# Splitting norm, statistics and last-square blocks of two attention layers into phases of a lane

## The chip, the cores and the metric

The program runs on one core of one Trainium2 chip. The core has five engines that work at the same time, each through an instruction queue of its own: TensorE (PE; matmuls and transposes into PSUM banks), VectorE (DVE), ScalarE (ACT; functions such as square root, Silu and exponential, and copies out of PSUM), GpSimd (POOL) and SyncE (SP; transfers). An instruction that needs another engine's result waits on a semaphore at the head of its own queue. The metric is the device time of one execution of the whole program in microseconds (us); lower is better.

## What is computed

The reference is four layers, each an attention and a feed-forward part, on 8 sequences of 512 rows of 128 columns. The change touches the first and the third attention. Both are gated "delta rules" over normed rows. Cut to what matters here:

```python
# first attention (4 heads of 32 columns; x is layer-normed)
q, k, v = silu(causal_conv(x @ Wq)), silu(causal_conv(x @ Wk)), silu(causal_conv(x @ Wv))
beta = sigmoid(x @ Wb)
q, k = l2norm(q), l2norm(k)                 # per row and head: x * rsqrt(sum(x * x))
kb, v = k * beta, v * beta
out = delta_rule_chunkwise(q, k, v, kb)     # triangular inverse per chunk, then a scan over chunks
short, long = fir(v_direct, 5 taps), fir(v_direct, 64 taps)
stats = [mean, var, abs_mean, l2] of each of (short, long, out, v_direct)   # per row and head
weights = softmax(gelu([x, stats] @ W1 + b1) @ W2 + b2)
x = x + rmsnorm(mix of the four branches by weights) @ Wo

# third attention (4 heads; q, k of 32 columns, v of 64)
q, k, v = silu(causal_conv(h @ Wq)), silu(causal_conv(h @ Wk)), silu(causal_conv(h @ Wv))
q, k = l2norm(q) * 32 ** -0.5, l2norm(k)
g, beta = -exp(A) * softplus(h @ Wa + dt), sigmoid(h @ Wb)
o = gated_delta_rule(q, k, v, g, beta)
x = x + (rmsnorm(o) * silu(h @ Wg)) @ Wo    # then a small feed-forward part
```

## The kernel before

The program is a row of stages, one for each attention or feed-forward part. All engines meet at the start of a stage. In an attention stage one unit of work is one sequence: 512 rows as four tiles of 128, on 128 partitions. Eight units go through **two lanes**: lane 0 takes units 0, 2, 4, 6 and lane 1 units 1, 3, 5, 7, so a stage consists of four pairs. Each lane has its own buffers and four PSUM banks (`b[0]` to `b[3]`).

What sets the order of the work is the function `weave`. Every engine has a generator for a unit (`pe`, `act`, `dve`, `pool` of a stage's class) that issues instructions and yields the name of a phase: what is issued before a `yield` belongs to the phase of that name. `weave` takes one phase of lane 0 and one phase of lane 1 in turn, with lane 0 one phase ahead (`lead=1`), the same on each engine. So between two phases of lane 0 an engine's queue holds exactly one phase of lane 1, which is the one before in the list. Each engine runs its queue in this order, and dependences between engines are waits for named steps (`wait_ge(*u.act.at("norms"))`).

In the first attention (`L0Attn`) the phases are stats, features, project, convolve, rows, keys, then for two pairs of chunks the delta rule (score, strict, left and right levels, turn, wt, u, out), then branches, squares, statistics, gate, hidden, logits, softmax, mix, out, end. The parts concerned are:

- **rows**. PE turns the three convolved tensors and the early v into rows (line 422, called from `pe`). ACT copies them (lines 1169 and 1171), squares keys and queries (1173, 1174), waits for DVE's sums and takes the root (1176). DVE waits for the key squares, reduces (1301), waits for the query squares, reduces (1303), multiplies v by beta (1306), waits for the root, and forms reciprocal (1308) and the products of keys and queries (1310, 1311, 1313; step `ready`). PE's transposes of the phase keys wait for `ready`; ACT copies those (1179, 1182) and moves the held product (1184), and then PE can form the scores (782) and, after the strict part, the levels (801, 809). In the phase convolve, DVE's four multiply-adds per tensor stand at lines 1294 and 1297, and ACT applies Silu (1165).
- **branches and squares**. In the phase branches ACT copies the short filter's rows (1203). In the phase squares it squares the four branches (1208), waits for all statistics, and takes the root of the lengths (1210). `statistics_dve` does four blocks of eight instructions (1385 to 1397), one block for each branch, all in the phase squares. PE turns the statistics, ACT copies them (1213), PE forms the gate's products (1128) and DVE adds (1346).

The third attention (`L2Attn`) has the same shape. Its rows phase has ACT's copies (2736, 2739), squares (2741, 2742) and root (2744), DVE's reductions (2846), v product (2852), reciprocal (2855) and products (2857 to 2860). Between convolve and rows lies a phase decays (ACT's exponential at 2732); keys has ACT's copies at 2747 and 2750 and DVE's weighing (2864, 2865), and the first phase of the delta rule starts with DVE's step masks (2869). At a unit's end, in the phase squares, ACT squares the output (2770) and takes the root (2772); DVE reduces (2904), applies the gates (2908), and scales (2910, 2912). Then PE turns the rows and projects (2685), and DVE adds (2917).

## Time and profile before

| what | value |
|---|---|
| median of 3 runs | 5995.02 us (5983.47 to 5996.26) |
| the profiled execution: its own time, and its span | 5991.27 us, 5989.9 us |
| PE busy | 4244.2 us, 71% of the span |
| DVE busy | 2997.1 us, 50% |
| ACT busy | 1940.4 us, 32% |
| POOL busy | 817.9 us, 14% |
| share of the chain that ended last | PE 50%, DVE 29%, ACT 12% |
| first attention, about 28 to 1060 us | PE 790.2, DVE 484.1, ACT 311.4 us busy of 1032; mean granted clock 0.55 |
| third attention, about 2880 to 3920 us | PE 709.2, DVE 552.4, ACT 326.5 us busy of 1040; mean granted clock 0.62 |

No engine is busy for the whole span, so the shares say little alone. The way to read this profile is by stage, and in a stage by place: a row of the timeline gives the start and the duration of a merged group of instructions, its engine, line and shapes, and in brackets how long the engine had been idle before it and what ended that. The granted clock is a share of 2.4 GHz: 0.5 is 1.2 GHz.

### The profile page before, as it was taken

The numbers are of one execution on the slowest core, as the hardware profiler recorded it, in microseconds if no ns is written. First come the engines' busy times: TensorE is split into PE (matmuls) and PEld (weight loads), VectorE is DVE, ScalarE is ACT, GpSimd is POOL, SyncE is SP. The second block draws the span as 40 slices with busy tenths as digits, with TensorE's granted clock in tenths as the row PEclk, the third lists the DMA queues.
The fourth block names the chain that finished last, engine by engine and source line by source line (L and its number), as shares of the span: only waits on it lengthen the run. The fifth ranks groups of instructions, "written<-read, shape, count | busy, mean of one in ns | idle before, by whom it ended". The sixth has DMA issues, their size and how long they took to land.

```text
span 5989.9 us, 94866 instructions
## 1 busy us (share of the span) xinstructions
PE 4244.2 (71%) x39740; PEld 3259.9 (54%) x39740; DVE 2997.1 (50%) x7965; ACT 1940.4 (32%) x4236; POOL 817.9 (14%) x600
## 2 busy tenths in 40 slices
PE   6786968467888888855485766857777677776288
PEld 5574947345655555544374655734444445445277
DVE  4445363335455555565446555465555555555333
ACT  2233132123333333311323233234444444442122
POOL 0000000221100111124200000011111111110443
PEclk6555555688789988866666666668887788778599
DMA  9100000230000000011200000000000000000265
GB/s 261 41 2 1 2 1 2 87 119 1 1 1 1 1 1 1 1 35 19 48 2 1 1 1 1 2 1 1 1 1 1 1 1 1 1 1 1 67 167 139
DMA packets 140861, 152.33 MB, mean 25 GB/s; under 512 B 7809, under 2 KB 128003, under 8 KB 139793
## 3 DMA queue, kind: packets, MB, share of 16 engines
q1 hardware_dynamic: 119024, 128.21, 7.4%
q0 software_dynamic: 21408, 18.05, 1.8%
q8 instruction: 313, 5.13, 0.4%
q14 instruction: 116, 0.94, 0.1%
HBM read 87.38 MB, written 59.76 MB: 25 GB/s over the span
## 4 chain that ended last, share of the span: by engine, by line
PE 50%; DVE 29%; ACT 12%; issue 3%; POOL 2%; DMA 2%; another core or an unknown queue 1%; SPq 0%; DVEq 0%; POOLq 0%; ACTq 0%
PE banks_lane L801 4%; ACT work L3231 4%; PE banks_lane L422 3%; PE banks_lane L3668 2%; PE banks_lane L1885 2%; PE banks_lane L3073 2%; PE banks_lane L1251 2%; PE banks_lane L809 2%; PE banks_lane L3117 2%; PE banks_lane L950 1%; DVE weights L3324 1%; ACT work L1979 1%; PE banks_lane L3152 1%; DVE work L2793 1%
## 5 line engine op out<-in xcount | busy, mean ns | idle before, releaser
L422 PE MATMUL banks_lane<-constants,work 128*128 128x128 f32 x968 | 203.9, 361 | 513.7 <-DVE work L408 231.5
L422 PEld LDWEIGHTS banks_lane<-constants,work 128*128 128x128 f32 x968 | 155.9, 187 | 587.2 <-DVE work L408 222.6
L402 POOL TENSOR_TENSOR weights<-weights,constants 128x4 f32<-128x4 f32 x76 | 78.5, 1033 | 2088.9 <-DVE weights L397 2088.9
L422 PE MATMUL banks_lane<-constants,weights 128*128 128x128 f32 x596 | 124.5, 347 | 336.3 <-DVE weights L408 98.0
L3231 ACT ACTIVATE work<-banks_lane,weights 128x192 f32<-128x192 f32 (+1 forms) x512 | 248.2, 499 | 245.9 <-DVE weights L3328 245.9
L422 PEld LDWEIGHTS banks_lane<-constants,weights 128*128 128x128 f32 x596 | 88.6, 178 | 369.6 <-issue 169.7
L3336 POOL TENSOR_TENSOR weights<-weights,constants 128x16 f32<-128x16 f32 x64 | 185.4, 2896 | 531.0 <-DVE weights L3244 531.0
L402 POOL TENSOR_TENSOR work<-work,constants 128x4 f32<-128x4 f32 x76 | 77.3, 1018 | 1192.3 <-DVE work L397 1192.3
L3152 PE MATMUL banks_lane<-constants,work 128*128 128x128 f32 x896 | 149.5, 316 | 120.5 <-DVE work L3316 70.7
L3152 PEld LDWEIGHTS banks_lane<-constants,work 128*128 128x128 f32 x896 | 113.1, 160 | 150.3 <-DVE work L3316 89.0
L2032 DVE TENSOR_REDUCE work<-banks_lane 128x2 f32<-128x512 f32 x256 | 158.8, 683 | 67.7 <-PE banks_lane L1899 67.3
L3324 DVE TENSOR_REDUCE weights<-banks_lane 128x2 f32<-128x384 f32 (+1 forms) x256 | 121.9, 518 | 114.6 <-PE banks_lane L3139 114.1
L1979 ACT ACTIVATE work<-banks_lane 128x384 f32<-128x384 f32 (+1 forms) x256 | 118.5, 550 | 174.9 <-PE banks_lane L1920 106.9
L3080 PE MATMUL banks_lane<-constants,weights 128*128 128x128 f32 x256 | 68.4, 419 | 139.1 <-DVE weights L3255 82.6
L3668 PE MATMUL banks_lane<-weights,work 128*128 128x256 f32 x624 | 143.1, 382 | 14.7 <-DVE weights L3710 14.7
L3167 PE MATMUL banks_lane<-work 128*64 128x128 f32 x1792 | 127.8, 284 | 34.0 <-ACT work L3193 34.0
L656 POOL DMA_INDIRECT out<-weights,chunk_places x78 | 121.5, 1557 | 194.4 <-DVE chunk_places L648 127.3
L569 POOL DMA_INDIRECT room_l_ffn<-weights,indices x96 | 92.6, 965 | 397.3 <-DVE weights L392 341.3
L3073 PE MATMUL banks_lane<-weights,work 128*128 128x512 f32 x192 | 145.0, 918 | 0.0
L801 PE MATMUL banks_lane<-work 64*64 64x32 f32 x2048 | 124.2, 293 | 23.4 <-DVE work L891 19.6
L1885 PE MATMUL banks_lane<-weights,work 128*128 128x128 f32 x1024 | 135.5, 297 | 5.9 <-ACT work L2001 5.9
L1885 PEld LDWEIGHTS banks_lane<-weights,work 128*128 128x128 f32 x1024 | 131.3, 211 | 10.3 <-ACT work L2001 10.3
(779 smaller groups left out, 11145.2 us busy)
## 6 DMA issues: line engine op xcount, KB each, us to landing
work<-experts_dram_l_ffn SPq DMA_DIRECT2D x39, 964.0 KB
room_l_ffn<-work SPq DMA_DIRECT2D x30, 1188.0 KB, 15.1
work<-experts_dram_l_ffn SPq DMA_DIRECT2D x23, 512.0 KB
weights<-weights_dram SPq DMA_DIRECT2D x1, 4833.5 KB, 14.3
work<-room_l_ffn SPq DMA_DIRECT2D x36, 132.0 KB, 3.2
weights<-weights_dram SPq DMA_DIRECT2D x1, 4112.0 KB, 12.7
weights<-bands_dram SPq DMA_DIRECT2D x1, 4096.0 KB, 13.1
weights<-room_l_ffn SPq DMA_DIRECT2D x26, 132.0 KB, 4.4
```

The source lines that it names most:

```text
L402: pool.tensor_tensor(n.rstd, n.rstd, c("neghalf", cols=(0, n.rstd.shape[1])), ALU.pow).then_inc(*u.pool.step(name))
L422: done = pe.transpose(bank[0:rows, t * P:(t + 1) * P], block, c("ident"))
L801: made = pe.matmul(b[2][g, m * SMALL:(m + 1) * SMALL], self.strict[g, m, :], self.x[g, m, :])
L1885: made = pe.matmul(b[1][:, cols_of(t)], m.ff[:, f, cols_of(t)], self.w(u, f"down{f}"), start=f == 0, stop=f == L1_ATTN_FF - 1)
L1979: act.activation(m.probs[:, hh, 0:blocks, :].rearrange("p b q -> p (b q)"), b[hh][:, 0:blocks * P], ACT.Exp, scale=L1_ATTN_SCALE).then_inc ...
L2032: dve.tensor_reduce(m.top[r][:, :, hh, L1_ATTN_HD], b[hh][:, :].rearrange("p (t c) -> p t c", t=2), AX, ALU.max, negate=True).then_inc(*u. ...
L3073: pe.matmul(b[n][:, :], m.xT[:, cols_of(t)], self.w(u, "qkv", cols=(n * L2_FFN_INNER, (n + 1) * L2_FFN_INNER))).then_inc(*u.pe.step(f"proj ...
L3152: made = pe.transpose(u.banks[2 + side][:, cols_of(hh)], m.probs[n % 2][:, hh, side * P:(side + 1) * P], self.c("ident"))
L3231: act.activation(m.probs[n % 2][:, hh, L2_FFN_BACK + lo:2 * P], u.banks[side][:, j * span:(j + 1) * span], ACT.Exp, scale=m.q_factor[:, t, ...
L3324: dve.tensor_reduce(m.top[:, t, 4 * group + side:4 * group + 4:2], u.banks[side][:, 0:2 * span].rearrange("p (j c) -> p j c", j=2), AX, AL ...
L3336: pool.tensor_tensor(m.rn[:, t, :, :], m.rn[:, t, :, :], c("neghalf", cols=(0, 2 * L2_FFN_HEADS)).rearrange("p (n h) -> p n h", n=2), ALU. ...
L3668: made = pe.matmul(bank[:, g * CHUNK:(g + 1) * CHUNK], self.w(u, f"{name}{f}", cols=(g * P, (g + 1) * P)), m.z[:, f, :], start=f == 0, sto ...
```

## The change

Only `yield` statements are added, at the same places of all four engines' generators. No instruction is added, removed or altered, except for table loads of ACT, which the build puts in where the function changes.

- In both attentions rows becomes three phases: **squared** (PE's transposes, ACT's copies and squares), **summed** (DVE's two reductions and the v product, ACT's root) and **rows** (DVE's reciprocal and products).
- In the first attention squares is preceded by four phases **branch0** to **branch3**: DVE's statistics of one branch in each; ACT's four squares all lie in branch0, and its root stays in squares.
- In the third attention squares is preceded by **out squares**, which holds ACT's squares of the output.

```diff
# L0Attn.pe
         turn(pe, u, c, b[0], [m.vT[:, t * P:(t + 1) * P] for t in range(TILES)], "v_early")
+        yield "squared"
+        yield "summed"
         yield "rows"
...
         yield "branches"
+        for n in range(len(m.branches)):
+            yield f"branch{n}"
         yield "squares"
# L0Attn.act
         act.activation(flat(m.kb), flat(m.qrow), ACT.Square).then_inc(*u.act.step("q_squares"))
+        yield "squared"
         act.wait_ge(*u.dve.at("sums"))
         act.activation(m.rn, m.ss, ACT.Sqrt).then_inc(*u.act.step("norms"))
+        yield "summed"
         yield "rows"
...
             act.activation(m.squares[n], flat(src), ACT.Square).then_inc(*u.act.step(f"squares{n}"))
+        for n in range(len(m.branches)):
+            yield f"branch{n}"
         act.wait_ge(*u.dve.at("statistics"))
# L0Attn.dve
         yield "convolve"
+        yield "squared"
         dve.wait_ge(*u.act.at("k_squares"))
...
         dve.tensor_tensor(heads_of(m.vb), heads_of(m.vrow), by_beta, ALU.mult).then_inc(*u.dve.step("vb"))
+        yield "summed"
         dve.wait_ge(*u.act.at("norms"))
...
-        self.statistics_dve(dve, u)
+        yield from self.statistics_dve(dve, u)
# L0Attn.statistics_dve, in the loop over the branches
             dve.scalar_tensor_tensor(var, m2, 1.0 / DK, m1, ALU.mult, ALU.subtract).then_inc(*u.dve.step("statistics"))
+            yield f"branch{n}"
# L2Attn.act
         act.activation(m.kT, m.krow, ACT.Square).then_inc(*u.act.step("squares1"))
+        yield "squared"
         act.wait_ge(*u.dve.at("sums"))
         act.activation(m.rn, m.ss, ACT.Sqrt).then_inc(*u.act.step("norms"))
+        yield "summed"
         yield "rows"
...
         act.activation(m.vrow, m.orow, ACT.Square).then_inc(*u.act.step("out_squares"))
+        yield "out squares"
         act.wait_ge(*u.dve.at("out_sums"))
# L2Attn.dve
         yield "decays"
+        yield "squared"
         for n, squares in enumerate((m.kb, m.kT)):
...
+        yield "summed"
         dve.wait_ge(*u.act.at("norms"))
...
+        yield "out squares"
         dve.wait_ge(*u.act.at("out_squares"))
```

The generators of PE and POOL get the same names without content, except that PE's transposes now lie in squared.

How the change moves instructions is seen in the order of the queues. First VectorE's queue in the first attention, where the two lanes' norms begin (`done_ACT_lane0` is a wait for ScalarE's work of lane 0). Before, lane 0's reductions, reciprocal and products stand ahead of lane 1's convolution (lines 1294 and 1297):

```order
L1301 TENSOR_REDUCE weights<-work 128x16 [waits done_ACT_lane0]
L1303 TENSOR_REDUCE weights<-work 128x16 [waits done_ACT_lane0]
L1306 TENSOR_TENSOR work<-weights 128x512 [waits done_DVE_lane0]
L1308 RECIPROCAL weights<-weights 128x32 [waits done_ACT_lane0]
L1310 TENSOR_TENSOR work<-work,weights 128x512 [waits done_DVE_lane0]
L1311 TENSOR_TENSOR work<-work,weights 128x512
L1313 TENSOR_TENSOR work<-work,weights 128x512 [waits done_DVE_lane0]
L1294 TENSOR_SCALAR work<-work,weights 128x512 [waits done_ACT_lane1]
L1297 SCALAR_TENSOR_TENSOR work<-work,weights 128x512 [waits done_DVE_lane1] x3
```

The same place of the same queue after the change (the lines are numbered anew: 1294 is now 1302, 1301 is 1310, 1308 is 1318), from lane 1's last convolution on:

```order
L1302 TENSOR_SCALAR work<-work,weights 128x512 [waits done_ACT_lane1]
L1305 SCALAR_TENSOR_TENSOR work<-work,weights 128x512 [waits done_DVE_lane1] x3
L1310 TENSOR_REDUCE weights<-work 128x16 [waits done_ACT_lane0]
L1312 TENSOR_REDUCE weights<-work 128x16 [waits done_ACT_lane0]
L1315 TENSOR_TENSOR work<-weights 128x512 [waits done_DVE_lane0]
L1318 RECIPROCAL weights<-weights 128x32 [waits done_ACT_lane0]
L1320 TENSOR_TENSOR work<-work,weights 128x512 [waits done_DVE_lane0]
L1321 TENSOR_TENSOR work<-work,weights 128x512
L1323 TENSOR_TENSOR work<-work,weights 128x512 [waits done_DVE_lane0]
L1310 TENSOR_REDUCE work<-work 128x16 [waits done_ACT_lane1]
L1312 TENSOR_REDUCE work<-work 128x16 [waits done_ACT_lane1]
```

Lane 1's whole convolution has moved ahead of lane 0's reductions, and lane 1's own reductions follow lane 0's products.

Second, ScalarE's queue in the third attention, from lane 0's last square to lane 1's root. Before:

```order
L2742 ACTIVATE work<-work 128x512
L2744 ACT_TABLE_LOAD
L2744 ACTIVATE weights<-weights 128x32 [waits done_DVE_lane0]
L2732 ACT_TABLE_LOAD
L2732 ACTIVATE work<-banks_lane 128x36 [waits done_PE_lane1]
L2747 COPY work<-banks_lane 128x512 [waits done_PE_lane0]
L2750 COPY work<-banks_lane 128x4x128 [waits done_PE_lane0] x2
L2736 COPY work<-banks_lane 128x4x128 [waits done_PE_lane1] x2
L2739 COPY work<-banks_lane 128x512 [waits done_PE_lane1] x2
```

After the change (2742 is now 2756, 2744 is 2759, 2732 is 2746, 2736 is 2750, 2747 is 2763):

```order
L2756 ACTIVATE work<-work 128x512
L2746 ACT_TABLE_LOAD
L2746 ACTIVATE work<-banks_lane 128x36 [waits done_PE_lane1]
L2759 ACT_TABLE_LOAD
L2759 ACTIVATE weights<-weights 128x32 [waits done_DVE_lane0]
L2750 COPY work<-banks_lane 128x4x128 [waits done_PE_lane1] x2
L2753 COPY work<-banks_lane 128x512 [waits done_PE_lane1] x2
L2755 ACTIVATE work<-work 128x512 [waits done_ACT_lane1]
L2756 ACTIVATE work<-work 128x512
L2759 ACTIVATE work<-work 128x32 [waits done_DVE_lane1]
L2763 COPY work<-banks_lane 128x512 [waits done_PE_lane0]
```

Lane 1's exponential stands ahead of lane 0's root, lane 1's copies and squares stand ahead of lane 0's copies of the keys, and lane 1's root has no load of its own. ScalarE's queue has 2773 rows before and 2765 after: four loads fewer in each of the two attentions.

## Rows read from the trace of the kernel before

**Rows 1.** Vector engine idle before line 1301, whole kernel: releaser, us in total, times.
```profile
  ACT work L1173: 45.7, 8
```

**Rows 2.** First attention, units 2 and 3, timeline: start, us, engine, line, operation [idle before].
```profile
308.41 1.54 ACT L1158 COPY work<-banks_lane 128x512 f32<-128x512 f32 x3
...
314.09 0.69 DVE L1301 TENSOR_REDUCE weights<-work 128x16 f32<-128x512 f32 x1 [6.25 <-ACT work L1173]
...
316.15 0.35 DVE L1308 RECIPROCAL weights<-weights 128x32 f32<-128x32 f32 x1
...
318.48 0.48 DVE L1294 TENSOR_SCALAR work<-work,weights 128x512 f32<-128x512 f32 x1
```

**Rows 3.** The same timeline, from lane 1's last Silu to the first level.
```profile
326.88 0.63 ACT L1165 ACTIVATE weights<-work 128x512 f32<-128x512 f32 x1 [2.13 <-DVE work L1297]
327.42 0.57 ACT L1179 COPY work<-banks_lane 128x512 f32<-128x512 f32 x1
...
329.42 0.60 ACT L1169 COPY weights<-banks_lane 128x512 f32<-128x512 f32 x1
...
329.69 2.11 PE L782 MATMUL banks_lane<-work 32*128 32x256 f32 x16 [0.16 <-ACT work L1184]
...
331.74 2.08 PE L1078 MATMUL banks_lane<-work,weights 128*128 128x512 f32 x2
...
332.18 0.69 DVE L1301 TENSOR_REDUCE work<-work 128x16 f32<-128x512 f32 x1 [5.19 <-ACT work L1173]
...
336.71 2.83 PE L422 MATMUL banks_lane<-constants,work 128*128 128x128 f32 x12 [2.89 <-DVE work L1313]
...
341.01 2.11 PE L782 MATMUL banks_lane<-work 32*128 32x256 f32 x16 [1.48 <-ACT work L1184]
...
343.06 1.92 PE L801 MATMUL banks_lane<-weights,work 64*64 64x32 f32 x32
```

**Rows 4.** Windows (length, PE, PEld, DVE, ACT, POOL busy, PEclk, DMA, GB/s).
```profile
310.00:320.00 10.00, 4.32 (x26) 3.25 (x25) 5.68 (x10) 7.33 (x11) 0.00 (x0) 0.77 0.00 0
...
360.00:380.00 20.00, 20.00 (x462) 19.37 (x460) 3.91 (x10) 0.00 (x0) 0.00 (x0) 0.50 0.01 2
```

**Rows 5.** Third attention, the rows' norms of units 2 and 3, timeline.
```profile
3225.17 0.23 ACT L2744 ACTIVATE weights<-weights 128x32 f32<-128x32 f32 x1
3225.42 1.28 ACT L2732 ACT_TABLE_LOAD   x1
3226.11 0.35 DVE L2855 RECIPROCAL weights<-weights 128x32 f32<-128x32 f32 x1
...
3226.71 0.20 ACT L2732 ACTIVATE work<-banks_lane 128x36 f32<-128x36 f32 x1
...
3232.04 0.69 DVE L2864 TENSOR_TENSOR work<-work,weights 128x512 f32<-128x512 f32 x1 [3.26 <-ACT work L2750]
...
3235.73 0.69 DVE L2846 TENSOR_REDUCE work<-work 128x16 f32<-128x512 f32 x1 [2.39 <-ACT work L2741]
...
3240.78 1.29 DVE L2869 TENSOR_TENSOR weights<-constants,weights 128x512 f32<-128x512 f32 x2
```

**Rows 6.** First attention, the branches' statistics of units 2 and 3, timeline.
```profile
506.42 0.69 DVE L1385 TENSOR_REDUCE work<-work 128x16 f32<-128x512 f32 x1 [0.91 <-ACT work L1203]
...
507.70 2.09 PE L1128 MATMUL banks_lane<-weights 32*128 32x512 f32 x8 [0.68 <-ACT weights L1213]
...
508.21 0.69 DVE L1389 TENSOR_REDUCE work<-work 128x16 f32<-128x512 f32 x1 [0.51 <-ACT work L1208]
...
517.77 2.48 DVE L1346 TENSOR_TENSOR weights<-banks_lane,work 128x512 f32<-128x512 f32 x4
```

**Rows 7.** Third attention, the last squares of units 0 and 1, timeline.
```profile
3137.83 1.22 DVE L2904 TENSOR_REDUCE weights<-work 128x16 f32<-128x1024 f32 x1 [0.57 <-ACT work L2770]
...
3144.61 3.78 PE L2685 MATMUL banks_lane<-weights,work 128*128 128x128 f32 x16 [0.78 <-ACT work L2776]
...
3149.43 0.68 DVE L2917 TENSOR_TENSOR weights<-weights,banks_lane 128x512 f32<-128x512 f32 x1
```

More of the change, by code:

```diff
@@ L1424, in pool @@
         yield "stats"
-        for phase in ("features", "project", "convolve", "rows", "keys"):
+        for phase in ("features", "project", "convolve", "squared", "summed", "rows", "keys"):
             yield phase
@@ L1428, in pool @@
             yield from delta_phases(pair)
-        for phase in ["branches", "squares", "statistics", "gate", "hidden", "logits", "softmax", "mix",
+        for phase in ["branches", *(f"branch{n}" for n in range(4)), "squares", "statistics", "gate", "hidden", "logits", "softmax", "mix",
                       "out", "end"]:
@@ L2843, in dve @@
         yield "decays"
+        yield "squared"
         for n, squares in enumerate((m.kb, m.kT)):
@@ L2853, in dve @@
                           ALU.mult).then_inc(*u.dve.step())
+        yield "summed"
         dve.wait_ge(*u.act.at("norms"))
@@ L2902, in dve @@
                 yield f"out{chunk}"
+        yield "out squares"
         dve.wait_ge(*u.act.at("out_squares"))
@@ L2940, in pool @@
         yield "affine"
-        for phase in ("features", "project", "convolve", "decays", "rows", "keys"):
+        for phase in ("features", "project", "convolve", "decays", "squared", "summed", "rows", "keys"):
             yield phase
@@ L2945, in pool @@
             yield from delta_phases(pair)
+        yield "out squares"
         yield "squares"
```

## The prediction

> **What bounds the kernel now.** I read the stage windows first, then the timeline of the two places that the change touches, then the idle time of the lines in them. No engine bounds this program throughout: in the first and third attention two lanes share every engine, each engine works its own queue strictly in written order, and the time is the chain of hand-overs. So the question is where an engine stands at the head of its queue on a wait while ready work of the other lane is queued behind it. One such place is large. VectorE waits 45.7 us in eight waits for ScalarE's squares of the keys [rows 1], 6.25 us each in lane 0 and 5.19 us each in lane 1 [rows 2, 3]; 4 x 6.25 + 4 x 5.19 = 45.8, so the four pairs of units are alike and one pair can be worked out and multiplied by four. During lane 0's wait all of lane 1's convolution could run: its first input is copied at 308.4 + 0.6 = 309.0, yet it starts at 318.48, since lane 0's block, with its two waits inside, is one phase [rows 2]. Afterwards PE is full in the delta rule (20.00 of 20 us in one stretch [rows 4]), so what is won before its entry cannot hide there: the full stretch starts earlier as a whole.
>
> **Part 1, first attention, rows' norms.** The convolution of lane 1 took 318.48 to 326.88 where Silu starts, 8.4 us [rows 2, 3]. It now starts at 309.0 and ends at 317.4. Its last Silu (0.63) ends at 318.1. ScalarE then needs a table load (1.28 [rows 5]) for lane 0's root: 319.4, root done 319.6. Lane 0's sums, 1.4 us from 317.4, and its v product are done by then. From its reciprocal to the end of its products VectorE took 318.48 - 316.15 = 2.3 us [rows 2], so with a hand-over of 0.1 on either side lane 0 is ready at 322.1, which is 3.5 us **later** than now.
>
> Lane 1 gains more. Its four copies follow the root at 319.6. From the first copy to its key reduction it took 332.18 - 329.42 = 2.8 us [rows 3], so the reduction starts at 322.4, when VectorE has just finished lane 0's products (322.0). Its root needs no load now, since lane 0's root came last, and follows the sums at about 323.9 to 324.1. From the reduction to its transposes took 336.71 - 332.18 = 4.5 us [rows 3]: lane 1 is ready at 326.9 instead of 336.7.
>
> Entry of the delta rule. Lane 0's four ScalarE moves before its scores took 329.69 - 327.42 = 2.3 us [rows 3]; they now stand behind lane 1's root: 324.1 + 2.3 = 326.4 for the scores, whose transposes (322.1 + 2.8) are done. The scores and lane 1's held product take 2.1 and 2.0 us [rows 3], so lane 1's transposes start at 330.4; their data is ready since 326.9. From there to lane 1's scores took 341.01 - 336.71 = 4.3 us: 334.7. Lane 0's first level stood at 343.06, right behind those scores, 2.05 us after their start: now 336.7. The gain is **6.4 us a pair, 25.6 us in four**. The cover for lane 0's later readiness is lane 1's chain, which still ends last at the entry: lane 0's scores stand 10.3 us ahead of its first level, and its own work in between is less than the 13.4 us of today. Bounds for a pair: 5.2 if each hand-over is some 0.1 us longer than the rows' and the early transposes delay the held product by 0.6; 9 if the clock helps (below).
>
> A rule of the Trainium skill speaks against this. The rows show a root from 3225.17 for 0.23 us, the next load at 3225.42 for 1.28 us and its function at 3226.71: no gap on either side [rows 5]. "ScalarE: Activation LUTs", under "What ACT_TABLE_LOAD costs", adds a drain of about 1.38 us to each 1.28 us load. By it lane 0's root, and all behind it, would come 1.4 us later: 5.0 a pair. By the rows, 6.4; I take the rows. What the order of instructions shows is that one load disappears per pair in each of the two stages, eight in all; what they give is in the chain above and is not counted again.
>
> **Part 2, first attention, the branches.** Today lane 1's first statistics wait 0.91 us for its own copy, which stands behind lane 0's root on ScalarE, and 0.51 us for the square [rows 6]. With the branches alternating both are done in time: **1.4 us a pair, 5.7 in four**. The same 64 instructions run otherwise. Lane 0's last statistics come 5.4 us later (two of lane 1's blocks of 2.7 lie ahead of them), so its gate products begin at 507.7 + 5.4 = 513.1 [rows 6]; VectorE reaches them at 517.77 - 1.4 = 516.4, so they stay hidden with 3 us to spare. Bounds: 0 and 1.5.
>
> **Part 3, third attention, rows' norms.** VectorE's idle time decides. After lane 0's norms it idles 3.26 and 2.39 us [rows 5]. New: lane 0's root has two loads ahead of it, since lane 1's exponentials move before it. Squares end at 3225.17 - 1.28 = 3223.9; load, exponential and load (1.28 + 0.2 + 1.28) and the root (0.23) give 3226.9, where VectorE arrives at 3226.1 [rows 5]: 0.8 idle. It ends the products 2.4 later, at 3229.4. Lane 1's 16 transposes start at 3225.4, take 16 x 2.83 / 12 = 3.8 [rows 3], and copy and square bring its reduction to about 3230.4: 1.0 idle. The reductions and the v product are 3240.78 - 3235.73 - 2.3 = 2.7 us [rows 5], to 3233.2; lane 0's three copies, behind lane 1's root at 3232.3, end at 3234.0: 0.7 idle. The saving is 5.65 - 2.5 = 3.15 us a pair, **12.6 us in four**, and the step masks at 3240.78 start at 3237.6. Bounds: 1.5 (a further wait behind the root) and 4.5 (idle only once).
>
> **Part 4, third attention, last squares.** Lane 1's last three small instructions go ahead of lane 0's reduction at 3137.83. They end about 0.9 us after that start. Lane 0's projection then ends at 3144.61 + 3.78 + 0.9 = 3149.3; VectorE came to it at 3149.43 [rows 7]. Lane 1 itself is finished sooner, but waits there. I take **0.1 us a pair, 0.4**; bounds -1 and +1 a pair.
>
> **Sum.** 25.6 + 5.7 + 12.6 + 0.4 = 44.3 us. Against the profiled execution (5991.3 us, of which the span is 5989.9) that is 5947.0; the median of the runs shown lies 3.7 us higher, at 5995.0, and gives **5950.7 us**.
>
> **Rivals.**
> *TensorE runs faster at the entry.* The granted clock was 0.77 on average between 310 and 320 us, so at its upper level of 2.4 GHz for half of it, and 0.50, 1.2 GHz, in the delta rule [rows 4]. The transposes and products of both lanes now follow each other from 316.5 to 333 us with few gaps, where PE idled before. If the upper level lasts into lane 1's transposes and scores (2.83 and 2.11 us, halved) it saves 2.5 us a pair in the first attention: 10 us, 5941. Against it: scores and held product filled 329.69 to 333.8, and the transposes at 336.71 and scores at 341.01 were slow all the same [rows 3]. "TensorE: Matmul & The Clock Gate", part 1, says in the Trainium skill that the slow state is the default and that activity lifts it, which speaks for this rival. 0.16.
> *Loads cost more in the new order.* They now stand ahead of roots that nobody but they delay. If each costs twice the 1.28 us of rows 5, part 1, with one on its path, falls to 5.1 and part 3, with two, to 0.6 a pair: 20.4 + 5.7 + 2.4 + 0.4 = 28.9, 5966. The rows have no gap behind a load, which speaks against it. "ScalarE: Activation LUTs" of the Trainium skill, with its drain, speaks for it. 0.10.
> *The gain is given back.* If the delta rule, in which each lane's levels wait for the other's turn on PE, absorbs the earlier entry and only the other parts' 10 us or so remain, 5985. That PE is full there [rows 4] speaks against it. It is also what follows if the lanes were paced by something that the phases do not touch. 0.07.
> *Lane 0's delay is what counts.* It becomes ready 3.5 us later in the first attention, its keys are copied 2.0 us later in the third, its reduction 0.9 us later. If lane 0, not lane 1, were last at the entries: 4 x (3.5 + 2.0 + 0.9) - 5.7 = 20 us slower, 6015. It decides once lane 1 gains less than lane 0 loses; the rows give lane 1 9.8 us. 0.05.
> That the phases move nothing is excluded by the order of instructions.
>
> **How the numbers follow.** Forecast 0.62, faster clock 0.16, dearer loads 0.10, given back 0.07, lane 0 0.05. The first three and part of the fourth are faster by over 0.2% (12 us, about what a measurement of this kernel can tell from no change): faster 0.89, within 0.2% 0.06, slower 0.05. The range takes in the clock's case with some of part 3's upper bound, 5936, and the dearer loads, 5966, with a margin; it leaves out 0.12 and some tails.
>
> **What would show it.** Per pair of the first attention: the waits before the key reductions fall from 6.25 and 5.19 us to under 1; lane 0's products start 3.5 us later than now, counted from its own convolution; from lane 0's scores to its first level it takes 10.3 us instead of 13.4; the pair period falls by 7.8 us. Third attention: the pair's period falls by 3.2 us, with idle of about 1 us before three lines. Eight table loads fewer. Wrong would be: the granted clock higher in 316 to 340, a wait of ScalarE on a root that holds the other lane's copies by over 1 us, or a period that doesn't fall though the waits do.

## The result, and the profile after

| | before | after |
|---|---|---|
| median of 4 runs each | 5989.52 us (5983.47 to 5996.26) | 5933.58 us (5918.74 to 5936.99) |
| ratio, 95% interval | | 0.9902, 0.9879 to 0.9924 |
| profiled execution, its span | 5991.27 us, 5989.9 us | 5931.01 us, 5929.7 us |
| mean granted clock | 0.737 | 0.741 |

The change is faster by 1.0%, some 56 us by the medians. The forecast was 5950.7 us with a range from 5936; the time lies 17 us below the forecast and 2.4 us below the range. The order of the hand-overs came out as forecast; the size was too small, mainly because TensorE's granted clock rose at the delta rule's entry, which the forecast had only as a rival. One execution of `e8_after_again` (below) took 6154.65 us at a mean granted clock of 0.646; every ratio leaves it out.

The page of the changed kernel, first its span, the busy times and the shares of the chain that ended last:

```profile
span 5929.7 us, 94809 instructions
...
PE 4230.7 (71%) x39691; PEld 3256.4 (55%) x39740; DVE 2998.1 (51%) x7965; ACT 1929.4 (33%) x4228; POOL 818.7 (14%) x600
...
PE 51%; DVE 29%; ACT 12%; issue 3%; POOL 3%; DMA 2%; SPq 0%; DVEq 0%; POOLq 0%; ACTq 0%
```

These rows hardly tell where 60 us went: the shares are those of before to a point. ScalarE is busy for 11.0 us less, most of it the eight table loads (8 x 1.28 = 10.2), and TensorE for 13.5 us less (4244.2 to 4230.7). Part of that can be the 49 matmuls whose records this trace lacks; but line 422's 968 transposes of `work` alone, all there in both, went from 203.9 to 193.7 us, a first sign that some of them run faster. The rest is less standing still. The waits of the two rows sections are what changed. VectorE's idle time before the key reductions, 45.7 us in eight waits before [rows 1], is now this (the line is 1310 after the change):

```profile
  ACT work L1177: 0.8, 4
```

The timeline of the first attention, units 2 and 3, from lane 0's reduction to the first level; this answers to [rows 2] and [rows 3]. The pair begins 9.22 us sooner here (its first copy at 286.86 instead of 296.08), so 9.22 is to be taken off a time of before for a comparison:

```profile
308.08 0.68 DVE L1310 TENSOR_REDUCE weights<-work 128x16 f32<-128x512 f32 x1
...
310.40 0.35 DVE L1318 RECIPROCAL weights<-weights 128x32 f32<-128x32 f32 x1 [0.32 <-ACT weights L1181]
...
312.87 1.60 PE L422 MATMUL banks_lane<-constants,work 128*128 128x128 f32 x12
...
313.00 0.69 DVE L1310 TENSOR_REDUCE work<-work 128x16 f32<-128x512 f32 x1 [0.19 <-ACT work L1177]
...
316.73 2.11 PE L782 MATMUL banks_lane<-work 32*128 32x256 f32 x16 [2.26 <-ACT work L1190]
318.77 1.66 PE L1080 MATMUL banks_lane<-work,weights 128*128 128x512 f32 x2
...
320.04 1.68 ACT L856 COPY work<-weights 32x256 f32<-32x256 f32 x4
320.27 1.48 PE L422 MATMUL banks_lane<-constants,work 128*128 128x128 f32 x12
...
321.74 0.59 ACT L1185 COPY work<-banks_lane 128x512 f32<-128x512 f32 x1
...
324.17 1.17 PE L782 MATMUL banks_lane<-work 32*128 32x256 f32 x16 [2.42 <-ACT work L1190]
325.27 1.12 PE L801 MATMUL banks_lane<-weights,work 64*64 64x32 f32 x32
```

Two things are to be seen. The idle times of 6.25 and 5.19 us are gone (no bracket, and 0.19). And the last three rows of TensorE are short: lane 1's turns, scores and first level take 1.48, 1.17 and 1.12 us where they took 2.83, 2.11 and 1.92 [rows 3]. The windows say why, first two of the kernel before over that place, then two of the changed kernel (length, then busy time of each engine, the granted clock third from the end):

```profile
326.00:336.00 10.00, 6.09 (x26) 3.45 (x26) 4.62 (x10) 9.00 (x19) 0.00 (x0) 0.50 0.01 2
336.00:346.00 10.00, 7.81 (x71) 6.68 (x71) 6.10 (x16) 6.20 (x15) 0.00 (x0) 0.50 0.00 1
```

```profile
310.00:320.00 10.00, 7.61 (x37) 4.60 (x36) 7.52 (x16) 6.91 (x17) 0.00 (x0) 0.68 0.01 2
320.00:330.00 10.00, 6.30 (x149) 5.22 (x147) 6.51 (x17) 6.72 (x17) 0.00 (x0) 1.00 0.01 2
```

Before, TensorE's granted clock was 0.50 (1.2 GHz) from 326 to 346 us; after, it is 1.00 (2.4 GHz) from 320 us on, where lane 1's turns start. The prediction had named a higher granted clock at this place as a sign of being wrong. Lane 0's scores, at 316.73 behind 2.26 us of idle time, still took the 2.11 us of the lower clock.

The third attention, units 2 and 3, answers to [rows 5]:

```profile
3183.42 0.69 DVE L2864 TENSOR_REDUCE weights<-work 128x16 f32<-128x512 f32 x1 [3.29 <-ACT work L2755]
...
3185.44 1.28 ACT L2759 ACT_TABLE_LOAD   x1
...
3186.74 0.23 ACT L2759 ACTIVATE weights<-weights 128x32 f32<-128x32 f32 x1
...
3187.00 0.35 DVE L2874 RECIPROCAL weights<-weights 128x32 f32<-128x32 f32 x1 [0.76 <-ACT weights L2759]
...
3190.53 0.69 DVE L2864 TENSOR_REDUCE work<-work 128x16 f32<-128x512 f32 x1 [1.13 <-ACT work L2755]
...
3193.97 0.69 DVE L2883 TENSOR_TENSOR work<-work,weights 128x512 f32<-128x512 f32 x1 [0.34 <-ACT work L2766]
...
3197.50 1.29 DVE L2888 TENSOR_TENSOR weights<-constants,weights 128x512 f32<-128x512 f32 x2
3198.33 3.75 PE L2666 MATMUL banks_lane<-weights,constants 128*128 128x512 f32 x4 [6.86 <-DVE weights L2888]
```

The idle times of 3.26 and 2.39 us became 0.76, 1.13 and 0.34, against 0.8, 1.0 and 0.7 foretold. The root follows its load at once (3185.44 + 1.28 = 3186.72, root at 3186.74). From the first reduction to the step masks takes 14.08 us; before it was 17.41.

The branches' statistics of units 2 and 3 answer to [rows 6]. Shown are the ends and starts of blocks in the middle of the eight:

```profile
480.30 0.18 DVE L1407 SCALAR_TENSOR_TENSOR work<-weights 128x16 f32<-128x16 f32 x1
480.41 0.69 DVE L1395 TENSOR_REDUCE work<-work 128x16 f32<-128x512 f32 x1
...
482.91 0.19 DVE L1407 SCALAR_TENSOR_TENSOR work<-work 128x16 f32<-128x16 f32 x1
483.00 0.68 DVE L1395 TENSOR_REDUCE weights<-work 128x16 f32<-128x512 f32 x1
...
496.05 2.48 DVE L1356 TENSOR_TENSOR weights<-banks_lane,work 128x512 f32<-128x512 f32 x4
```

Neither wait of lane 1 is left, and from the first block (474.29) to the gate's add takes 21.76 us; before, 493.90 to 517.77, 23.87.

The last squares, [rows 7], in the changed kernel, units 0 and 1:

```profile
3106.30 3.78 PE L2699 MATMUL banks_lane<-weights,work 128*128 128x128 f32 x16 [0.78 <-ACT work L2793]
...
3110.12 0.69 DVE L2937 TENSOR_TENSOR weights<-weights,banks_lane 128x512 f32<-128x512 f32 x1 [2.22 <-PE banks_lane L2699]
```

VectorE now waits 2.22 us for the projection: it comes there sooner, and the projection does not.

Laid side by side, by the stages of the profiled executions: the first attention took 1039.1 us and takes 998.3 (from its first copy to its last add of x); the third 987.3 and 976.7. Together that is 51 of the 60 us between the two spans. Another 13.3 us lie in a stretch that the change does not touch, the fourth layer's attention and the routing behind it: from the end of the third layer's feed-forward part (line 3306 before) to the fourth's first expert product (line 3661) it is 233.4 us in the profiled execution of before, 220.1 in that of the changed kernel, and 219.5 to 221.2 in those of all twelve other kernels of this study. The remaining stretches together take some 4.5 us more. So the 60 us between the two profiled executions overstate the change.

### The profile page after: what moved, and what is told of

It reads as the page before. It is cut to its first block, busy times and chain, and to the rows that moved or that the text cites. A ratio compares the mean times of both kernels' runs of the same rounds, so it can differ in the third digit from the quotient of the medians.

```text
span 5929.7 us, 94809 instructions
## 1 busy us (share of the span) xinstructions
PE 4230.7 (71%) x39691; PEld 3256.4 (55%) x39740; DVE 2998.1 (51%) x7965; ACT 1929.4 (33%) x4228; POOL 818.7 (14%) x600
## 4 chain that ended last, share of the span: by engine, by line
PE 51%; DVE 29%; ACT 12%; issue 3%; POOL 3%; DMA 2%; SPq 0%; DVEq 0%; POOLq 0%; ACTq 0%
ACT work L3252 4%; PE banks_lane L801 4%; PE banks_lane L422 3%; PE banks_lane L3689 2%; PE banks_lane L1896 2%; PE banks_lane L3094 2%; PE banks_lane L1259 2%; PE banks_lane L809 2%; PE banks_lane L3138 2%; PE banks_lane L950 1%; DVE weights L3345 1%; ACT work L1990 1%; PE banks_lane L3173 1%; POOL room_l_ffn L569 1%; DVE work L2810 1%
## 5 line engine op out<-in xcount | busy, mean ns | idle before, releaser
L422 PE MATMUL banks_lane<-constants,work 128*128 128x128 f32 x968 | 193.7, 345 | 457.2 <-DVE work L408 229.6
L865 ACT COPY weights<-weights 32x256 f32<-32x256 f32 x32 | 12.9, 404 | 374.3 <-DVE weights L906 373.9
```

Source lines behind the costliest of these rows:

```text
L422: done = pe.transpose(bank[0:rows, t * P:(t + 1) * P], block, c("ident"))
```

## The experiments

The kernels numbered 1 to 4, 5 to 8 and 9 to 11 each ran on one chip together with the kernel before; each ratio is to those runs of before. Besides the whole, intervals of the trace are compared for the four pairs of a stage, since most of them repeat to a few hundredths. In the first attention a pair is measured from its first copy (line 1154 before).

**One part at a time.** The first four kernels each have one part of the change.

`e1_rows0`, the rows' phases of the first attention:

```diff
# L0Attn pe, act, dve, pool: between convolve and rows
+        yield "squared"
+        yield "summed"
```

> The kernel before with the norm block of the first attention alone split into squared, summed and rows. Theory A (order of hand-overs as in part 1 of the prediction, plus a faster PE clock at the delta rule's entry): the entry comes 6.4 us earlier by order and about 2 us more in those pairs whose last scores run in 1.2 us instead of 2.1 us; the stage gains 32 to 36 us. Theory B (order alone; what was missed lies elsewhere): 25.6 us, and the scores take 2.1 us in all pairs. Theory C (part 1's chain was wrong by more than the clock): the gain is outside 24 to 37 us.

Measured: 5949.96 us, ratio 0.9944 (0.9926 to 0.9961). The first attention takes 1000.5 us, 38.6 less. First levels stand 37.5, 38.3, 38.4 and 38.4 us after the pair's start, against 46.97 in every pair of before. So this part alone is worth more than the 25.6 us of the forecast: 8.6 to 9.5 us a pair by the first level instead of 6.4, 35.3 in four. The stage's 38.6 us lie just above the 37 us that had been set as the upper end of theories A and B; the whole (0.9944, 33.5 us) and the first levels lie within. The remaining 3.3 us fell behind the levels, where one trace differs from the next by as much (below).

`e2_branches`, the branches' phases alone:

```diff
# L0Attn, statistics_dve, in the loop over the branches (and the same names for pe, act, pool)
+            yield f"branch{n}"
```

> The kernel before with the first attention's statistics alone split into branch0 to branch3. Part 2 of the prediction: 1.4 us a pair, 5.7 us in all, with the two idle times of 0.91 and 0.51 us gone. A rival in which the split also gives PE or ScalarE work earlier would give over 8 us.

Measured: 5977.38 us, ratio 0.9988 (0.9974 to 1.0002); the whole cannot tell it from no change. The interval can: from the first block to the gate's add it is 21.74 or 21.75 us in all four pairs instead of 23.87, and the first attention takes 8.2 us less. That is 2.1 us a pair where 1.4 was forecast, and the 8.2 us reach the rival's bound of 8, by which TensorE or ScalarE would have to gain as well. `e9_one_split` below finds the excess on VectorE itself.

`e3_rows2`, the rows' phases of the third attention:

```diff
# L2Attn pe, act, dve, pool: between decays and rows
+        yield "squared"
+        yield "summed"
```

> The kernel before with the norm block of the third attention alone split. Part 3 of the prediction: 12.6 us; after's own trace shows 17.41 - 14.08 = 3.3 us a pair from lane 0's first reduction to its step masks, so 13.3 us by that. The rival, that some of it is given back later in the stage, puts it at about 10.6 us, which is what the stage as a whole gained between the two traces.

Measured: 5972.29 us, ratio 0.9980 (0.9967 to 0.9993). From the first reduction to the step masks 14.08 us in all four pairs, 3.33 less than before (3.15 forecast).

`e4_out`, the last squares alone:

```diff
# L2Attn pe, act, dve, pool: ahead of squares
+        yield "out squares"
```

> The kernel before with the third attention's last squares alone split off. Part 4 of the prediction: 0.4 us faster, that is no difference; what each stage that the edit does not touch varies from one execution to the other is seen best here. If the part costs, as its later reduction of lane 0 could, up to 4 us slower.

Measured: 5981.23 us, ratio 0.9992 (0.9976 to 1.0007). The interval from lane 0's reduction of the output squares (line 2904 before) to its add of the projection shrinks from 11.6 to between 10.3 and 10.6 us because it begins later. Counted from the squares themselves, the add comes 12.2 to 12.6 us behind them instead of 12.4 to 12.7, in the changed kernel too. It is worth what was forecast, next to nothing.

The four ratios multiply to 0.9904, against 0.9902 for the whole. Each ratio is uncertain by 0.0013 to 0.0018, and as far as that can tell, the parts add up; what has to be explained is the size of the first two.

**The clock at the entry.** In the changed kernel the products behind the held product are fast. Either that is the cause of the excess, or a companion of it. `e5_warm_before` gives the kernel before nothing of the change, only work for TensorE in the idle time ahead of its turns:

```diff
# L0Attn.pe, before: in keys, behind the held product
+        for _ in range(12):
+            pe.transpose(b[0][:, 0:P], c("ident"), c("ident"))
```

> The kernel before, with 12 dummy transposes of the identity added in each lane of the first attention, behind the held product and ahead of the products of the key squares; their result is overwritten unread, so no output depends on them. They lie in TensorE's idle time ahead of its turns (4.0 us for lane 0, 2.9 for lane 1 in the kernel before). Nothing of the order of the other engines changes. If the excess of the rows part over the forecast (8.6 to 9.6 us a pair instead of 6.4) is TensorE's granted clock at the entry, which no longer falls because the idle time is shorter: lane 1's turns last about 1.5 us instead of 2.83, its scores 1.2 instead of 2.11 and the first level's product 1.1 instead of 1.92 in most pairs, the first level starts about 2 us sooner after the start of a pair (45 instead of 46.97), and four pairs give 8 to 12 us, a ratio of 0.998 to 0.9987. If the excess comes from the order on VectorE and ScalarE alone, the durations stay at 2.83, 2.11 and 1.92 or the level does not move: ratio 1.000, level at 47.

Measured: 5974.59 us, ratio 0.9986 (0.9973 to 0.9999). The second pair's entry in that kernel (line 1080 is the added work; the pair begins 1.59 us sooner than before's):

```profile
330.14 2.07 PE L1078 MATMUL banks_lane<-work,weights 128*128 128x512 f32 x2
332.01 2.57 PE L1080 MATMUL banks_lane<-constants 128*128 128x128 f32 x12
335.11 1.53 PE L422 MATMUL banks_lane<-constants,work 128*128 128x128 f32 x12 [0.53 <-DVE work L1315]
338.23 1.17 PE L782 MATMUL banks_lane<-work 32*128 32x256 f32 x16 [1.59 <-ACT work L1186]
339.33 1.12 PE L801 MATMUL banks_lane<-weights,work 64*64 64x32 f32 x32
```

and its windows there:

```profile
336.00:338.00 2.00, 0.64 (x6) 0.40 (x4) 1.90 (x7) 1.98 (x4) 0.00 (x0) 1.00 0.00 0
338.00:340.00 2.00, 1.77 (x40) 1.47 (x40) 0.43 (x2) 0.72 (x4) 0.00 (x0) 1.00 0.00 0
```

With TensorE idle for 0.53 us instead of 2.89 ahead of the turns, the granted clock is 1.00 where it was 0.50, and the same products take 1.53, 1.17 and 1.12 us. First levels stand at 46.04, 44.84, 44.86 and 44.85 us instead of 46.97. In the 20 pairs of the five traces that have the old entry and no added work, the level stands between 46.0 and 47.0, so 44.85 is not one of their values. Adding work made the kernel before faster. That is the clock's effect by itself, 2.1 us a pair in three of four and 0.9 in the first, 7.3 us in all. The first attention as a whole takes 1027.1 us, 11.9 less than before; the other 4.6 us fell behind the first levels, and no run shows whether they belong to the added work.

`e6_warm_after` asks whether more of it is to be had in the changed kernel, ahead of lane 0's scores:

```diff
# L0Attn.pe, after: between rows and keys
+        if u.lane == 1:
+            pe.wait_ge(*u.act.at("v_early"))
+            for _ in range(10):
+                pe.transpose(b[0][:, 0:P], c("ident"), c("ident"))
```

> The changed kernel, with 10 dummy transposes of the identity added in lane 1 of the first attention, after v's first copy and ahead of its held product; overwritten unread. They fill TensorE's idle 2.3 us ahead of lane 0's scores. If the clock at the entry is what lane 0's scores (2.1 us) pay for: these become 1.2 us, the fourth pair's first level, 39.04 in the changed kernel, comes to 38.4 or below, and four pairs gain 2 to 4 us against the changed kernel (ratio 0.9895 against the kernel before). If the clock there is set by what ran earlier, or the copies that follow end last anyway: the level stays at 37.7 to 39.0 and the ratio at 0.990.

Measured: 5926.71 us, ratio 0.9918 (0.9901 to 0.9934), against 0.9909 for the changed kernel on the same chip. Lane 0's scores take 1.17 us in all four pairs, as they should, and the first levels stand at 37.46, 37.79, 37.47 and 38.40. That is 0.6 us a pair better than the 37.68, 38.41, 39.04 and 38.39 of the changed kernel, and does not show in the time. With the same added work `e10_warm_both` (below) has its levels at 38.40, 38.42, 38.41 and 38.40: nothing is won. Its second pair tells why (lane 0's scores, lane 1's turns, scores and first level):

```profile
312.42 1.17 PE L782 MATMUL banks_lane<-work 32*128 32x256 f32 x16 [1.24 <-ACT work L1194]
...
314.49 1.47 PE L422 MATMUL banks_lane<-constants,work 128*128 128x128 f32 x12
318.92 2.12 PE L782 MATMUL banks_lane<-work 32*128 32x256 f32 x16 [2.96 <-ACT work L1194]
320.97 1.92 PE L801 MATMUL banks_lane<-weights,work 64*64 64x32 f32 x32
```

Lane 0's scores are fast, and lane 1's, behind 2.96 us of idle time instead of 2.42, are slow in their place. Both count. In the seven traces with the new entry the level stands at 37.46 or 37.47 us in the three pairs where turns and both scores are fast (1.17 us), and at 38.39 to 38.42 in all seventeen pairs where one of the two scores takes 2.11 or 2.12 us. Lane 0's scores count through ScalarE, which copies them and forms the strict part (the row at 320.04 above ends at 321.72) before it copies lane 1's keys (321.74).

**The third attention's handover.** Ahead of the step products TensorE is idle for 6.86 us and then runs them in 3.75 us (the row at 3198.33 above). `e7_warm_between`:

```diff
# L2Attn.pe, after: in between, where the first pair of chunks has no wait of its own
             if pair > 0:
                 pe.wait_ge(*u.dve.at("got1"))
+            else:
+                for _ in range(16):
+                    pe.transpose(b[3][:, 0:P], c("ident"), c("ident"))
```

> The changed kernel, with 16 dummy transposes added at the handover of the third attention, ahead of TensorE's wait for the step masks of the first lane; overwritten unread. They fill 6.9 us of idle TensorE. By the clock theory the products behind the wait take about 1.9 us instead of 3.75 and a pair gives up to 1.5 us more than the changed kernel (6 us in all, ratio 0.989). By its rival, that VectorE and ScalarE set the end of this stretch, the products are quicker and the lane's first level starts no sooner: ratio 0.990.

Measured: 5912.22 us, ratio 0.9893 (0.9873 to 0.9912). The products behind the added work (line 2666 here; the step products are 2669):

```profile
3194.69 1.98 PE L2669 MATMUL banks_lane<-weights,constants 128*128 128x512 f32 x4 [0.93 <-DVE weights L2891]
```

They take 1.98 us instead of 3.75 (3.34 in the first pair), the scores come 3.97 us after the masks in all four pairs (5.4, 6.9, 7.0 and 7.0 in the changed kernel), and the first level comes 15.7 to 15.9 us after the masks (18.1 to 19.6 in the changed kernel). So the rival that VectorE and ScalarE hold this stretch anyway has fallen. The whole stage takes 949.7 us in this trace, 27 less than the changed kernel, more than the clock theory had promised (6); up to the first level it is 3.4 us a pair, some 14. `e10_warm_both` (these transposes and those of `e6_warm_after`) and `e11_warm_lane0` (only lane 0's sixteen, `elif u.lane == 0`) were to show what of that is firm.

> The changed kernel with both sets of dummy transposes, those ahead of lane 0's scores in the first attention and those ahead of the step products in the third; overwritten unread. If the gains add: the first attention's 991 us and the third's 950, ratio 0.9885 to the kernel before, some 20 us below the changed kernel. If the first set only moves work within its scatter: 0.9893, as with the second set alone.

> The changed kernel with the 16 dummy transposes of the third attention in lane 0 only. With them in both lanes a pair took 242.3 us instead of 246 to 252. If it is the 6.9 us of idle TensorE ahead of lane 0's step products that cost the clock: the first lane's products again take 1.98 us instead of 3.4, and most of the gain, 4 to 7 us a pair, stays. If lane 1's gap of 4.5 us costs as much: the pair lies half way, at 245 to 246 us.

Measured: 5917.24 us, ratio 0.9892 (0.9873 to 0.9911), and 5919.93 us in a single run. Their third attentions take 966.5 and 960.9 us. The first of the two has the very same third attention as `e7_warm_between`, 949.7 us, so single executions of it differ by 17 us. Nor is the higher clock certain: in both traces lane 0's step products take 1.98 or 1.99 us in two of four pairs only, and 3.54 and 3.56, or 3.09 and 3.56, in the others. A pair's period is 246.0 to 246.4 us in `e11_warm_lane0`, which its expectation had as the case where lane 1's gap counts as well; since `e10_warm_both` with both sets has 245.1, 249.6 and 245.3, the question whether lane 1's sixteen matter stays open. Three traces of the third attention as the change leaves it, with no work added there (the changed kernel's two and `e6_warm_after`), have 976.7, 978.6 and 974.1 us; the gain is 7 to 29 us. The first attention's set adds nothing to the third's, 0.9892 as against 0.9893. By whole times the versions with this added work stand at 0.9893 and 0.9892, the changed kernel at 0.9902 and 0.9909; the intervals overlap, so a faster version is likely, but not shown to the last.

`e8_after_again` is the changed kernel once more.

> The changed kernel again, unaltered, beside the others on the same chip. If the result of its first runs (5933.6 us, ratio 0.9902 to the kernel before) is the size of the change: ratio 0.989 to 0.9915, and the first attention again at 998 us with first levels at 37.7 to 39.0 us after a pair's start. If part of it was chance of one execution: nearer to the sum of the four parts run alone, 0.9904, or to the forecast, 0.9926.

Measured: 5924.9 us, the median of four executions, ratio 0.9909 (0.9889 to 0.9930). First attention 990.1 us, 8 less than in the first trace, first levels at 38.40, 38.10, 38.42 and 38.41; third attention 978.6. The size of the change is confirmed: the ratio lies within 0.001 of the first one and of the four parts' product.

**The branches' missing 0.7 us.** `e9_one_split` is the kernel before with only the first of the four new phases:

```diff
# L0Attn.statistics_dve, before (and one phase for pe, act, pool)
+            if n == 0:
+                yield "branch0"
```

> The kernel before with one phase branch0 alone, behind the first of the four statistics blocks. VectorE's queue keeps its old order (four blocks of lane 0, then four of lane 1), while ScalarE's copy and squares of lane 1 now stand ahead of lane 0's root, so lane 1's two waits (0.91 and 0.51 us) can go. It tells the two halves of the branches' gain apart, by the time from the first block to the first add of the gate, 23.87 us in the kernel before and 21.75 in the changed kernel. If alternation of the lanes at the block boundaries is worth the part that the forecast missed (a block that follows one of its own lane starts 0.22 us after the start of the last small operation ahead of it, one of the other lane's 0.09 to 0.11): 23.87 - 1.42 = 22.45 us. If the waits alone carry all of it: 21.75.

Measured: 22.27 us in all four pairs (a single run, 5976.81 us; its first attention takes 1033.0). This lies between the kernel before, 23.87, and the full split, 21.74, nearer to the 22.45 that the expectation gave for the case that alternation at the boundaries counts. Its blocks, where lane 0's last but one ends, where lane 0's last ends, and where lane 1's first ends (the reduction that follows is the next block's start):

```profile
498.21 0.18 DVE L1401 SCALAR_TENSOR_TENSOR work<-weights 128x16 f32<-128x16 f32 x1
498.44 0.69 DVE L1389 TENSOR_REDUCE weights<-weights 128x16 f32<-128x512 f32 x1
...
500.93 0.19 DVE L1401 SCALAR_TENSOR_TENSOR work<-weights 128x16 f32<-128x16 f32 x1
501.04 0.69 DVE L1389 TENSOR_REDUCE work<-work 128x16 f32<-128x512 f32 x1
...
503.54 0.18 DVE L1401 SCALAR_TENSOR_TENSOR work<-work 128x16 f32<-128x16 f32 x1
503.76 0.69 DVE L1389 TENSOR_REDUCE work<-weights 128x16 f32<-128x512 f32 x1
```

A block behind one of its own lane starts 0.22 or 0.23 us after the start of the small operation ahead of it, since each block waits for its own lane's last result; behind one of the other lane 0.11. The working is below.

## Why the prediction fell short

**The base.** The forecast took 44.3 us off a median of three runs, 5995.0. With one more run that median is 5989.5, and beside the experiments, over 35, 17 and 11 runs, 5986.6, 5980.8 and 5979.8. That accounts for 5.5 of the 17.1 us of the miss; the other 11.6 are terms of the sum. Taken off 5989.5, the forecast would be 5945.2 and the range would begin at 5930.5, below what was measured; that the time fell outside the range hangs on the base, the wrong terms do not. The profiled execution was no better base: it holds 12 to 14 us in an untouched stretch that no other trace shows.

**Part 1, the order: right.** Put in us after the pair's first copy, step by step:

| step of the second pair | before | forecast | after |
|---|---|---|---|
| lane 0's key reduction | 18.01 | 21.3 | 21.22 |
| lane 0's turns (ready) | 22.54 | 26.0 | 26.01 |
| lane 1's key reduction | 36.10 | 26.3 | 26.14 |
| lane 0's scores | 33.61 | 30.3 | 29.87 |
| lane 1's turns | 40.63 | 34.3 | 33.41 |
| lane 1's scores | 44.93 | 38.6 | 37.31 |
| first level | 46.98 | 40.6 | 38.41 |

Lane 0 is ready later, as worked out, and lane 1 carries the gain. The order on VectorE and ScalarE came out within 0.2 us up to the reductions.

**Part 1, the sizes: the step that failed** is "From there to lane 1's scores took 341.01 - 336.71 = 4.3 us" and "right behind those scores, 2.05 us after their start", and ahead of them the scores and held product that "take 2.1 and 2.0 us". They carried over the durations of before, and those were durations at a granted clock of 0.50. Of the 2.2 us between 40.6 and 38.41, 0.43 lie ahead of lane 0's scores (ScalarE's moves began 0.4 us sooner), and the rest is TensorE: scores and held product 3.54 us instead of 4.0 (0.46), lane 1's turns to scores 3.90 instead of 4.3 (0.40), scores to level 1.10 instead of 2.05 (0.95; the sum is 0.05 over by rounding). So the clock's share in this pair is some 1.8 us.

This is the first rival, given 0.16 with 2.5 us a pair, and it is what happened, though it pays less than the rival's halves: of the 1.35 us that lane 1's turns save, 0.4 reach the scores, since ScalarE comes to copy the keys only at 321.74. `e5_warm_before` showed the clock's effect without the change, 2.1 us a pair in three of four. What the forecast held against it was that the turns and scores of before were slow although a stretch of products stood ahead; but there 2.89 us of idle TensorE lay between [rows 3], and the change removes just that idle time, as its own working said (turns at 330.4, with data ready since 326.9). The Trainium skill's rule in "TensorE: Matmul & The Clock Gate", part 1, that activity lifts the clock, agrees here in direction, with 1.00 against 0.50 where the idle time is filled; it should have weighed more than the rows of an arrangement that the change does away with. It is not the whole account: a stretch in which TensorE is full stays at 0.50 (last section).

The clock is not firm in every pair: the third pair of the changed kernel had fast turns, but slow scores and a slow level, and its first level at 39.04 is the latest of the four:

```profile
568.95 1.53 PE L422 MATMUL banks_lane<-constants,work 128*128 128x128 f32 x12
572.41 2.12 PE L782 MATMUL banks_lane<-work 32*128 32x256 f32 x16 [1.93 <-ACT work L1190]
```

**Part 2: right in place, too small.** 1.4 us a pair were forecast, 2.12 measured. The failed step is "the same 64 instructions run otherwise". The bracket of an idle time isn't all that a removed wait gives. In `e9_one_split` lane 1's first block begins 0.11 us after the start of the small operation ahead; before it was 1.09 (505.33 to 506.42), so 0.98 is won where the bracket says 0.91. The reduction of the squares follows the one ahead at 0.60, as everywhere, where it was 1.19 (507.02 to 508.21): 0.59, where the bracket says 0.51. Together that is 1.57 of the 1.60 measured. Then five of the seven boundaries between blocks change lane in the changed kernel, against one in `e9_one_split`. The four others give 0.11 to 0.13 us each, 0.5 in all, and 1.60 + 0.5 is the 2.12 measured. The forecast's bound of 1.5 lay below the value.

**Part 3: right.** 3.15 us a pair up to the step masks forecast, 3.33 measured, and a pair's period fell from 252.4 to 249.3 us. The stage as a whole gained 10.6 us (8.7 in the second trace) of the 12.6 + 0.4 forecast; the delta rule's stretch of one pair varies by several us from execution to execution (126 to 137 us in the kernels here), so the difference isn't read as a loss. On average the four traces with this part and no work added there have a stage 11.7 us shorter than the six without it.

**Part 4: right,** 0.1 forecast, 0.1 to 0.5 measured. The projection bounds it; VectorE's 2.22 us of waiting there are the cover.

**The other rivals.** Dearer loads: fallen, by the root 0.02 us behind its load where two loads stand in a row. The drain that the Trainium skill's "ScalarE: Activation LUTs" adds under "What ACT_TABLE_LOAD costs" is not seen; with it the idle time of 0.76 us would have been over 2. Given back: fallen in the main; from the first level to the statistics the pairs take 149.0 to 155.3 us (150.1 to 153.1 before), and 0.1 to 1.0 us a pair is lost between the gate's add and the end. Its 5985 did not follow from the sum: with part 1 absorbed the others still give 18.7 us, with part 3 as well 6.1, not 10. Lane 0's delay: fallen; it is 3.5 us late, as foretold, and nobody waits for it: lane 0's scores start behind ScalarE's moves, which follow lane 1's root.

Summed by the intervals: 8.6 us a pair up to the first level and 2.12 in the branches are 42.9, of which the first attention kept 40.8, against 31.3 forecast. That is 9.5 us more there; the third attention fell 2.4 short. In this one trace the two stages so give 51.4 us, 7.1 more than forecast; in the second trace of the changed kernel they give 49.0 + 8.7 = 57.7, 13.4 more. The 11.6 us of the medians lie between the two. Averages say it best: the changed first attention takes 998.3, 990.1, 992.3 and 995.3 us in the four traces that have it as it is, 44.9 less than the 1038.9 of the three that have it as before. Of the 13.6 us beyond the 31.3 forecast, some 9 lie up to the first levels (about 7 by the clock) and 2.9 in the branches; the last 2 have no cause shown.

## What to carry to other kernels

Where two lanes share in-order queues, split a phase wherever it waits for another engine inside: the other lane's ready work then fills the wait, and it's no harm that the first lane is ready later as long as the second one ends the stretch. When a change closes idle time of TensorE, don't carry the durations of the products behind it over from the profile: look at the granted clock there, and work the sum out at both levels. And take the base from many runs; a profiled execution can hold a dozen us by chance in a stage that isn't in question.

## What the runs showed of the hardware

- Twelve useless transposes in TensorE's idle time brought the first levels of the kernel before forward by 7.3 us in four pairs, by the granted clock going from 0.50 to 1.00 at the products behind them in three. In the third attention sixteen did it for products that took 3.75 us after 6.86 us of idle, and 1.98 after the added work, in all four pairs of one trace and in two of four in each of two others.
- Added work can also just move the slow place: in `e10_warm_both` lane 0's scores went from 2.11 to 1.17 us and lane 1's, 6.5 us later, from 1.17 to 2.12, and the first level stayed at 38.4.
- A stretch in which TensorE is full with small products stays at a clock of 0.50 all the same, after the change as before [rows 4]:

```profile
360.00:380.00 20.00, 20.00 (x395) 19.14 (x395) 3.79 (x10) 5.31 (x13) 0.00 (x0) 0.50 0.01 2
```

- VectorE starts an operation that needs no result of the one ahead 0.13 us sooner than one that does (0.09 to 0.11 us after the start of the small operation ahead, against 0.22).
